# A Mamba stage on one core: GpSimd scales transposed input by B for four states a unit, and TensorE turns them into PSUM banks 0 and 1

## The reference, cut to what matters

```
xi, z  = split(x @ in_w.T);  xc = silu(conv4(xi) + conv_b)         # 256 channels
dt, B, C = split(xc @ xp_w.T);  delta = softplus(dt @ dtp_w.T + dtp_b)
for each of 16 states n, over time t:
    h[n] = h[n] * exp(delta * A[n]) + (delta * xc) * B[n]           # a scan over time
y = sum over n of h[n] * C[n], + xc * D;  out = (y * silu(z)) @ out_w.T
```

## Time and profile before

| | us |
|---|---|
| median of 3 runs | 2613.18 (2610.1 to 2615.79) |
| the profiled execution | 2614.2 |
| its span | 2612.1, 48904 instructions |
| busy: PE, DVE, ACT, POOL | 2227.8, 2240.6, 1895.3, 2198.4 |
| the states' stage, first to last L548 | 534.3 to 2083.2 |

### The profile page before, as it was taken

One profiled execution on the slowest core, in us unless ns is written; L12 is line 12 of the kernel. 1 busy time (PEld: TensorE's weight loads), 2 busy tenths in 40 slices (PEclk: granted clock), 3 DMA queues, 4 the chain that ended last, 5 costly groups with the idle time before them and its releaser, 6 DMA issues.

```text
span 2612.1 us, 48904 instructions
## 1 busy us (share of the span) xinstructions
PE 2227.8 (85%) x15840; PEld 1908.7 (73%) x15840; DVE 2240.6 (86%) x3430; ACT 1895.3 (73%) x3628; POOL 2198.4 (84%) x1402
## 2 busy tenths in 40 slices
PE   4899999668888898888888888888988768999992
PEld 3799999446776777776776766766766647999992
DVE  8766666789999999999999999999999887666666
ACT  4355555389999989999999999999999543555551
POOL 3677777379999999999999999999999936777772
PEclk8999999889999999999999999999999978999996
DMA  7011112533333333333333333333333240111126
GB/s 249 21 48 49 49 50 50 144 94 105 110 103 104 107 106 102 107 107 101 111 101 103 112 100 105 111 107 104 106 107 107 85 161 24 50 49 49 49 49 211
DMA packets 156821, 248.73 MB, mean 95 GB/s; under 512 B 22082, under 2 KB 66018, under 8 KB 155874
## 3 DMA queue, kind: packets, MB, share of 16 engines
q1 hardware_dynamic: 137568, 202.79, 26.1%
q0 software_dynamic: 18208, 37.26, 5.3%
q10 hardware_dynamic: 866, 6.43, 0.6%
HBM read 213.10 MB, written 33.29 MB: 94 GB/s over the span
## 4 chain that ended last, share of the span: by engine, by line
PE 37%; POOL 19%; DVE 15%; issue 14%; ACT 10%; DMA 4%; ACTq 0%; DVEq 0%; POOLq 0%; SPq 0%
PE bank L1351 10%; POOL buf L548 8%; DVE buf L917 7%; PE bank L1547 6%; PE bank L1372 6%; PE bank L1422 4%; POOL token_outputs L497 4%; POOL buf L487 4%; PE bank L1522 3%; PE bank L1332 3%; ACT over L1164 3%; DMA buf<-state_rows 2%; ACT scaled L1197 2%; DVE buf L904 2%; POOL buf L535 2%
## 5 line engine op out<-in xcount | busy, mean ns | idle before, releaser
L548 POOL TENSOR_TENSOR buf<-buf 128x1024 f32<-128x1024 f32 x512 | 1199.9, 2374 | 32.4 <-PE bank L1547 27.0
L917 DVE TENSOR_TENSOR_SCAN buf<-over,bank 128x512 f32<-128x512 f32 x832 | 953.8, 1200 | 4.9 <-PE bank L1522 2.7
L1164 ACT ACTIVATE over<-wgu,negA 128x510 f32<-128x510 f32 x832 | 541.5, 709 | 40.3 <-DVE buf L917 28.8
L1547 PE MATMUL bank<-id_sb,buf 128*128 128x128 f32 x4096 | 515.8, 279 | 6.8 <-POOL buf L548 6.8
L1547 PEld LDWEIGHTS bank<-id_sb,buf 128*128 128x128 f32 x4096 | 478.2, 144 | 57.2 <-issue 46.6
L1351 PE MATMUL bank<-parts 128*128 128x256 f32 x3408 | 447.6, 288 | 17.3 <-DVE buf L767 9.2
L1351 PEld LDWEIGHTS bank<-parts 128*128 128x128 f32 x3408 | 420.7, 193 | 36.7 <-issue 36.7
L1197 ACT ACTIVATE scaled<-wd_sb,I 128x256 f32<-128x256 f32 x896 | 377.3, 497 | 22.6 <-PE bank L1522 22.5
L497 POOL DMA_INDIRECT token_outputs<-buf,slot_out x284 | 299.5, 1055 | 87.9 <-issue 84.0
L487 POOL DMA_INDIRECT buf<-token_rows,slot_token x284 | 284.5, 1002 | 95.4 <-issue 82.5
L1522 PE MATMUL bank<-id_sb,scaled 128*128 128x128 f32 x1792 | 256.0, 280 | 88.3 <-ACT scaled L1197 38.2
(11 more groups left out here) (170 smaller groups left out, 3061.6 us busy)
## 6 DMA issues: line engine op xcount, KB each, us to landing
buf<-state_rows SPq DMA_DIRECT2D x608, 256.0 KB, 3.2
token_rows<-buf SPq DMA_DIRECT2D x32, 256.0 KB, 2.3
wd_sb<-token_outputs SPq DMA_DIRECT2D x16, 512.0 KB, 4.0
buf<-token_outputs SPq DMA_DIRECT2D x16, 512.0 KB, 4.8
buf<-token_rows,slot_token POOLq DMA_INDIRECT x284, 2.5
token_outputs<-buf,slot_out POOLq DMA_INDIRECT x284
out<-X SPq DMA_DIRECT2D x16, 256.0 KB, 3.6
wgu<-wgT ACTq DMA_DIRECT2D x1, 2048.0 KB, 9.1
```

What stands on the lines that cost most here:

```text
L548: pool.tensor_tensor(hC[:, b, :].rearrange("p (c w) -> p c w", c=C), hs[:, b, :].rearrange("p (c w) -> p c w", c=C), Cs[:, b, :].unsqueeze ...
L917: V.tensor_tensor_scan(hs[:, b, w], dA[:, b, c, :, :].rearrange("p s t -> p (s t)"), source, 0.0, ALU.mult, ALU.add).then_inc(s[f"scan_don ...
L1164: ins = A.activation(dA[:, n % R, c, :, 1:], delta[r][:, c * W:(c + 1) * W].rearrange("p (s t) -> p s t", s=S)[:, :, 1:], ACT.Exp, scale=n ...
L1547: ins = M.matmul(bank[4 + q // 2][:, at:at + P], hC[:, n % R, c * W + q * P:c * W + (q + 1) * P], id_sb[:, :], is_transpose=True, start=Fa ...
```

## The change

A fourth unit, 11, goes from the vector units to the pool units, and pool units are computed in another way. GpSimd no longer multiplies du by a broadcast row of B; it scales the transposed input duT by the column of B, four TENSOR_SCALARs of 128 x 256 into a new double buffer pscaled. TensorE transposes them back, eight blocks, into banks 0 and 1. ScalarE makes the decay of every state into dA, and VectorE scans all states with full scans. The fetches of B's rows and the half scans are gone. GpSimd's order is now 3, 9, 11 and 15 after times_C 0, 4, 6 and 9. turn_back_pool(n) stands at the head of TensorE's iteration n - 1. ScalarE's copy of duT and the last load of wd_sb wait for pscaled_done too.

```diff
-POOL_UNITS = (3, 9, 15)
+POOL_UNITS = (3, 9, 11, 15)
-MUL_AT = {0: 3, 4: 9, 11: 15}
-FETCH_C, FETCH_B, DECAY_LEAD = 3, 7, 3
+MUL_AT = {0: 3, 4: 9, 6: 11, 9: 15}
+FETCH_C, DECAY_LEAD = 3, 3
...
-        prod = carve(rest, 2 * CW).rearrange("p (b w) -> p b w", b=2)
-        Bs = carve(rest + 2 * CW, 2 * W).rearrange("p (b w) -> p b w", b=2)
+        pscaled = carve(rest, 2 * CW).rearrange("p (b q d) -> p b q d", b=2, q=G)
...
-            def product(p, r, n):
+            def scale_by_B(p, r, n):
                 u = p * 2 + r
                 turn = pool_before(u, n)
...
+                pool.wait_ge(s["BT_done"], u + 1)
+                pool.wait_ge(s["duT_done"], 2 * u + 2)
+                wait(pool, s["pturned1"], turn - 1)
+                for q in range(G):
+                    ins = pool.tensor_scalar(pscaled[:, turn % 2, q, :], duT[:, q, :], BT[:, u % 2, q, n:n + 1], None,
+                                             ALU.mult)
+                ins.then_inc(s["pscaled_done"], 1)
...
                         if n in MUL_AT:
-                            product(p, r, MUL_AT[n])
+                            scale_by_B(p, r, MUL_AT[n])
...
-                if on_pool(n):
-                    turn = pool_before(u, n)
-                    dve.wait_ge(s["pool_mul_done"], turn + 1)
-                    for c in range(C):
-                        dve.wait_ge(s[f"dP_ready{c}"], turn + 1)
-                        for q in range(S):
-                            w = slice(c * W + q * L, c * W + (q + 1) * L)
-                            ins = V.tensor_tensor_scan(hs[:, b, w], bank[c][:, q * L:(q + 1) * L],
-                                                       prod[:, turn % 2, w], 0.0, ALU.mult, ALU.add)
-                        ins.then_inc(s[f"scan_done{c}"], 1)
-                    return
-                dve.wait_ge(s["dA_ready"], decays_before(u, n) + 1)
+                dve.wait_ge(s["dA_ready"], N + 1)
...
+                    elif on_pool(n):
+                        dve.wait_ge(s[f"pturned{c}"], pool_before(u, n) + 1)
+                        source = bank[c]
...
+            def turn_back_pool(p, r, n):
+
+                u = p * 2 + r
+                turn = pool_before(u, n)
+                pe.wait_ge(s["pscaled_done"], turn + 1)
+                for c in range(C):
+                    wait(pe, s[f"scan_done{c}"], u * NS + n - 1)
+                    for q in range(G):
+                        ins = M.transpose(bank[c][:, q * P:(q + 1) * P], pscaled[:, turn % 2, q, c * P:(c + 1) * P],
+                                          id_sb[:, :])
+                    ins.then_inc(s[f"pturned{c}"], 1)
...
                     for n in range(NS):
                         if on_turn(n + 1):
                             turn_back(p, r, n + 1)
+                        elif n + 1 < NS and on_pool(n + 1):
+                            turn_back_pool(p, r, n + 1)
```

More of the change, by code:

```diff
@@ L101, in vector_before @@
     return (u + whole) * len(mine) + sum(m < part for m in mine)
-def decays_before(u, n):
-    return u * NSTATE + n - pool_before(u, n)
 def done(steps, name, turn):
@@ L316, in macaron_kernel @@
             experts_done expA_done dtp_zeroed diag_ready taps_spread taps_ready parts_ready skip_ready gT_pe gT_done BT_pe BT_done duT_pe duT_done scaled_done turned0 turned1 gated du_done dve_pre
-            act_pre pe_pre vareps_pre rstd_pre shift_pre res_done pe_post negA_done bcB_ready bc_copied bc_stored C_in0 C_in1 C_in2 C_in3 B_in0 B_in1 dA_ready
-            dP_ready0 dP_ready1 mul_done pool_mul_done scan_done0 scan_done1 hC_ready y_done""".split()
+            act_pre pe_pre vareps_pre rstd_pre shift_pre res_done pe_post negA_done bcB_ready bc_copied bc_stored C_in0 C_in1 C_in2 C_in3 dA_ready
+            pturned0 pturned1 mul_done pscaled_done scan_done0 scan_done1 hC_ready y_done""".split()
         s = {n: sem(n) for n in names}
@@ L383, in fetch_C @@
                              ).then_inc(s[f"C_in{n % R}"], DMA)
-            def fetch_B(u, r, n):
-                turn = pool_before(u, n)
[L387 to L392, removed]
             def pair_rows(p, last):
@@ L401, in pair_rows @@
                             fetch_C(u + 1, 1 - r, n + FETCH_C - NS)
[L402 to L406, removed]
                         if n == SP_AT["rows"] and not (last and r == 1):
@@ L412, in _ @@
                 fetch_C(0, 0, n)
-            fetch_B(0, 0, POOL_UNITS[0])
             pair_rows(0, False)
@@ L424, in _ @@
             sp.wait_ge(s["scaled_done"], turned_before(2 * NP, 0))
+            sp.wait_ge(s["pscaled_done"], pool_before(2 * NP, 0))
             sp.wait_ge(s["comb_done"], NG)
@@ L1167, in decay @@
                 ins.then_inc(s["dA_ready"], 1)
[L1169 to L1175, removed]
             def columns_of_B(u):
@@ L1187, in copy_duT @@
                     wait(act, s["scaled_done"], turned_before(u, 0))
+                    wait(act, s["pscaled_done"], pool_before(u, 0))
                 A.activation(duT[:, 2 * k:2 * k + 2, :], bank[7].rearrange("p (q d) -> p q d", q=2),
@@ L1235, in pair @@
                     for n in range(NS):
-                        if n + 1 < NS and on_pool(n + 1):
-                            decay_to_bank(p, r, n + 1)
                         beside(p, r, n, first, last)
                         if n + DECAY_LEAD < NS:
-                            if not on_pool(n + DECAY_LEAD):
-                                decay(p, r, n + DECAY_LEAD)
-                        elif prep and not on_pool(n + DECAY_LEAD - NS):
+                            decay(p, r, n + DECAY_LEAD)
+                        elif prep:
                             decay(pv, rv, n + DECAY_LEAD - NS)
```

## The result

| | before | after |
|---|---|---|
| median | 2613.88 us (2610.1 to 2615.79, 4 runs) | 3107.03 us (3105.71 to 3107.99, 4 runs) |
| ratio | | 1.1888, 95% interval 1.1868 to 1.1909 |
| span of the profiled execution | 2612.1 us | 3104.4 us |
| busy: PE, DVE, ACT, POOL | 2227.8, 2240.6, 1895.3, 2198.4 | 2460.3, 2208.6, 1901.2, 2438.1 |

The direction was forecast, the size was not: 2848 us, range 2735 to 2945. Of 493 us lost some 235 were foreseen.

A forecast was written before the change was run, and what follows sets the result against it. The gate-to-gate loop through GpSimd's row bounds the kernel. With the added wait a turn takes 47.3 + 4X = 55.7 us against 48.18, +234 over 31 turns and +1.4 for the first: 2848 us, range 2735 to 2945.

The forecast's parts named there:

- the loop from gate to gate: State stage: gate, C-product 4, GpSimd's unbroken row to C-product 15, sums, next gate set a turn, 48.18 us; chance 0.80.
- Scaling by GpSimd, X = 2.1 us a state: GpSimd's four TENSOR_SCALARs of 128x256 a state, 0.525 us each; 8.4 us a turn where three B-products took 7.0.
- rival C: GpSimd's scaling dearer than a two-input instruction's rate: X = 3.4, +12.7 us a turn, 3008 us; chance 0.05.
- The Trainium skill's rates: Documented GpSimd one-input rates, 1.03 or near 1.8 cycles an element: X 1.7 or 2.3, time about 2797 or 2873 us.
- The added wait, 2.33 + X + 4.83: TensorE's transposes of state 3 wait for GpSimd's scaling, holding convolution, sums and gate: 2.33 + X + 4.83 instead of 2.9 us.
- What lies after in a turn has slack: Later delta*input, 20.3 us after C-product 4 starts instead of 16.3, holds TensorE some 3 us; VectorE about 5 us ahead.
- Gate to C-product 4: Link over VectorE and TensorE: 10.8 us in a pair's first turn, 9.0 in its second, from 10.90 and 9.67.
- A: Rival: the loop does not lengthen, only GpSimd's own work counts, 49.3 us a turn, +1.1, 2648 us; chance 0.09.
- B: Rival: VectorE closes the turn and scalings are cheap; its saved 1.27 us product comes off each turn, 2574 us; chance 0.06.

The follow-up runs named there:

- experiment 2: Changed kernel, but GpSimd scales a state with one TENSOR_TENSOR of 128x1024, the column of B broadcast, instead of four TENSOR_SCALARs: 2828.39 us, 55.2 us a turn.
- experiment 4: Changed kernel, with TensorE's transposes of state 3 moved behind the sums of states 14 and 15: 2939.65 us, 58.9 us a turn.
- experiment 7: Changed kernel with two-operation scalings, state 3 scaled early and sum of state 0 in iteration 4: 2658.66 us; that sum move on the kernel before: 2607.74 us.
- experiment 1: Changed kernel, with several forms of GpSimd instructions added once ahead of the first scaling of the first turn to price each: 3141.72 us.
- experiment 8: Changed kernel with three pool units, 3, 9 and 15, unit 11 a vector unit again: 2967.42 us, 59.8 us a turn.
- experiment 5: Changed kernel, but GpSimd scales state 3 of the next turn after C-product 13 instead of after C-product 0: 2943.67 us, 58.9 us a turn.

## Why the prediction was right and wrong, step by step

- **What bounds the kernel, the loop from gate to gate:** right. The check of the first turn, 48.75, could not fail: its 2.9 us is what is left between C-product 15 and the gate of that same turn; only the second turn's 47.5 tests it. With the measured X of experiment 2 the same sum is 6 us off. Experiments 4 and 7 move its links and get 167 and 74 us back.
- **Scaling by GpSimd, X = 2.1 us a state, ends 1.25 and 2.9:** this is the step that failed. X was 3.6. I bounded an instruction with one input by one with two, as if the number of operands set the rate; experiment 1 shows a one-operation TENSOR_SCALAR of 256 columns slower (0.91 us) than a TENSOR_TENSOR of two full operands (0.69). The start of the next instruction, 0.22 us after L464, was read as the price at 16 columns, and L464's own 380 ns was left to rival C, with a chance of 0.05 and 3008 us, the nearest of all. The view of before that the earlier trace rows come from had the contrast that matters: there the two-operation TENSOR_SCALAR of 16 columns (L466) takes 205 ns, where L464 takes 380. The term was 4 x 1.5 = 6.0 us a turn too small, 186 us in all.

```profile
L466 POOL TENSOR_SCALAR SLf<-SLf 128x16 f32<-128x16 f32 x6 | 1.2, 205 | 0.5
```

- **The Trainium skill's rates** (GPSIMD Engine Reference, section 3.1), 1.03 and 1.8 cycles an element at 1.2 GHz: the one-operation form has a slope of 2.5 ns, 3.0 cycles, and follows neither. The two-operation form with a constant, 0.38 us for 256 columns with all fixed cost, comes to 1.8 cycles an element by the same clock. The Trainium skill (GPSIMD Engine Reference, section 4.1) calls one-input work roughly line rate; here the measurement decides against it for this form, which is slower than two-input work.
- **The added wait, 2.33 + X + 4.83 from C-product 15 to the gate:** the mechanism is right in every link. The last part took 6.3 us instead of 4.83 where TensorE's granted clock fell to 0.73 after the wait, and 4.67 where it stayed at 1.00. The mean of 30 turns is 6.06: 1.2 us a turn that no term had. Experiment 2 has both too: 6.38 us at 0.73 (1093.21 to 1099.59) and 4.66 at 1.00 (1150.38 to 1155.04), after waits of 2.64 and 2.66 us.
- **"What lies after in a turn has slack":** wrong by 1.2 us a turn. Delta*input now ends 27.1 us after C-product 4 starts (1286.96 against 1259.89), not the 22.6 that X = 2.1 gave, TensorE stands 4.6 us before it, and sum 11 is late for C-product 15: 0.47 and 1.52 us in the rows above, 1.2 on the mean. The price that was too low made this slack. Once the wait at the gate is out of the way, in experiment 4, this is the chain that closes the turn.
- **Gate to C-product 4, 9.0 and 10.8:** measured 8.89 and 10.74.
- **Sum of the misses:** 6.0 + 1.2 + 1.2 = 8.4 us a turn, as measured (64.1 - 55.7), 244 us over 29 intervals; the last two together are as forecast. The first gate comes 15.4 us later, where 1.4 was forecast: 14 more, some 6 of it the price of four scalings. That is 258, against 3107 - 2848 = 259.
- **Rivals:** A fell (TensorE does stand behind the scaling), B fell (experiment 8: the unit taken from VectorE pays nothing). C was right about the price, 3.4 for 3.6, and, at 3008 us, short of the two follow-on costs.

## What to carry to other kernels

Find the loop that closes a stage, and sort work by whether it lies in the loop or in the shadow of one of its links: by the sum of experiment 5 a scaling counts in full in GpSimd's unbroken row, while the product for state 3 before stood in no term of the loop; and one call, moved behind the sums of the same iteration, was worth 167 us. When a link is taken out, look for the next chain: in experiments 4 and 7 another wait stood in at once. A new wait at the head of an in-order queue costs what is queued behind it, and may lower TensorE's clock for that too. Where an instruction's price is unseen, bound it by its own form and count of operations, not by operands, and give the one odd row its weight.

## What was not expected of the hardware

- GpSimd's TENSOR_SCALAR with one operation runs at 2.5 ns a column; a second operation takes 256 columns from 0.91 to 0.46 us with a column (a multiplication by 1.0), and from 0.83 to 0.38 with a constant (an addition).
- A TENSOR_TENSOR of 1024 columns took 1.87 to 1.91 us on the transposed input and 2.33 us in the products by B and C. The runs do not say why.
- After waits of 3.34 us, the same to 0.01, TensorE's granted clock was 0.73 in one turn and 1.00 in another, and the same work took 6.3 or 4.67 us: slow in 25 of 30 turns. In experiment 2 it was slow behind 8 of 22 waits of 2.5 to 2.7 us, and behind none of 8 of 1.6 to 1.9. Before the change the same work, behind no such wait, ran at 1.00 in the stretch from 1119 to 1125 us.
